# Unread products in each round of layer 0, and new times and banks for the pieces of both layers

## The chip, the cores and the metric

One core of one Trainium2 chip runs the whole program. The metric is the device time of one execution in microseconds (us); lower is better. Before the change it was 1562.08 us, the median of three runs (1560.22 to 1565.09).

## What is computed

The input is 8 batches of 512 tokens of width 256, in fp32. Two transformer layers follow each other, each with two residual steps of a normalized branch:

```python
x = x + _layernorm(_L0_attn_ref(_layernorm(x, axis=-1), ...), axis=-1)
x = x + _layernorm(_L0_ffn_ref(_layernorm(x, axis=-1), ...), axis=-1)
x = x + _layernorm(_L1_attn_ref(_layernorm(x, axis=-1), ...), axis=-1)
x = x + _layernorm(_L1_ffn_ref(_layernorm(x, axis=-1), ...), axis=-1)
```

Layer 0 is causal attention with 16 heads of 16 and rotary positions, softmax with a true row maximum, an output product with bias, and then `silu(x @ wg.T) * (x @ wu.T)` times `wd` with 768 hidden columns. Layer 1 is causal attention with 16 heads of 64 whose scores go through `50 * tanh(s / 50)`, and then a mix of each token with the one before it, a sigmoid gate `r`, and `relu(k)**2` times a weight. Nothing of the result may be dropped: all products are of fp32 quality, each computed as three products of high and low halves (`product`, line 422).

## The kernel before, in words

**Pieces and rounds.** Each layer is a function (`phase1` for layer 0, the one behind it for layer 1). The work of one batch is cut into named pieces: `x_T` (transposes of the normalized input, line 1091), `rope`, `roped`, `turned`, `rope_sum`, `rope_hi`, `rope_lo` (queries and keys with rotary positions, and their halves), `place` (12 small DMAs that put a 64-row part into the operands `l_qT` and `l_kT`, line 761), `max` and `rmax` (a first pass of the scores, lines 1118 and 1125, whose row maxima DVE takes, lines 979 and 985), `maxT` and `maxT_out` (transposed maxima, line 1154), `maxima` (two DMAs that put them into `l_qT`, line 768), `score`, `tail` and `exp` (the scores again, line 1164, with their exponentials on ACT, line 897), `pv` (probabilities times values, line 1194), `pv_out` (its copy into `l_outT`, line 991), `outT` (transposed back, line 1203) and `outT_norm` (lines 996 and 999), `att_T` (line 1214), `o` and `o_out` (the output product, and the bias added on DVE, line 1017), the norms, `x1_T`, `gate`, `up`, `hidden`, `down`, `x2`, and the DMAs `load_x` (line 774), `store` (line 778) and `residual` (line 783). Scores of layer 1 are at line 1933, its query and key products split into halves by `qk_hi` (line 1665, ACT) and `qk_lo` (line 1750, DVE), and `L360` is where SP loads a weight of layer 1.

**What sets the order.** Each piece has a time in units (24 to a round) in a table written by hand, `table`. `Schedule` sorts the pieces of each engine by it. A piece's time divided by 24 says by how many rounds it lags behind its batch, so a round holds pieces of three or four batches. Rounds 3 to 6 are one hardware loop on each engine, whose order is that of `table`; the rounds before and after are written out, in the order of `moved_table`. `loading_table` and `prologue_table` order the weights' loading and splitting before each layer, and the prologue of layer 1 is interleaved with the last rounds of layer 0. In the profile a round of layer 0 takes about 80 us (rounds 3 to 6 lie in about 280 to 600) and one of layer 1 about 100 us. The tables give order alone: an engine's program is the sorted list, and only semaphores make it wait.

**Banks.** PSUM has eight banks, and `bank_table` names the one that each piece fills. `Banks` derives the waits: before PE fills a bank, `claim` makes it wait until the piece that filled it last has been read.

**Unread products.** `heat` multiplies a weight with itself into a bank that nobody reads:

```python
def heat(nc, out, w, count):
    for _ in range(count):
        nc.tensor.matmul(out, w[:, 0, 0:P], w[:, 0, 0:T], start=True, stop=True)
```

Before the change `warm` issues it 16 times with two products each while the first weights load, and layer 1 issues it nine times with six products each (`end_heat`), for the last batch. None is issued in the rounds between.

**Waits that matter here.** All DMAs of these pieces are issued by SP in one queue of its own order. `store` waits for `x2` (POOL, line 846); `residual` waits until the store of the batch before has landed, since both use `l_x`; DVE's addition of the residual (line 1030) waits for it. `maxima` waits for `maxT_out` on ACT, and PE's `score` waits until `maxima` has landed. `load_x` waits for both `x_T` of the batch before. A weight's load waits for a staging place, or in the prologue of layer 1 for room that layer 0 still holds.

Of the kernel before, what the change touches and what calls it, by code (L numbers as in the profile page):

```python
# [29 lines left out]
NC = D // P  # L30
# [413 lines left out]
def phase1(nc, block, ctx, memory, a, x_mid, tok, banks, psum, ident, expo):  # L444
# [56 lines left out]
    with nc.sbuf_tensor("l0_staging", [P, 2 * NM, T], F32, side="right") as raw:  # L501
# [21 lines left out]
        "rope_lo": {(0,): -6.92, (1,): -4.1, (2,): 3.46, (3,): 6.47},
        "place": {(0,): 1.92, (1,): 9.15, (2,): 16.42, (3,): 17.53},
        "v": {(0,): 9.07, (1,): 10.47},
        "v_out": {(0,): 10.27, (1,): 10.78},
        "max": {(0, 0): 2.31, (0, 1): 3.12, (1, 0): 3.69, (1, 1): 4.05, (2, 0): 6.471, (2, 1): 7.51, (3, 0): 7.73, (3, 1): 8.88, (4, 0): 13.38, (4, 1): 14.18, (5, 0): 15.1, (5, 1): 16.17, (6, 0): 18.88, (6, 1): 20.29, (7, 0): 20.74, (7, 1): 21.38},
        "rmax": {(0, 0): 2.58, (0, 1): 2.81, (1, 0): 3.44, (1, 1): 4.55, (2, 0): 7.24, (2, 1): 7.7, (3, 0): 8.1, (3, 1): 9.14, (4, 0): 13.04, (4, 1): 13.17, (5, 0): 14.54, (5, 1): 15.68, (6, 0): 17.52, (6, 1): 21.61, (7, 0): 22.25, (7, 1): 22.65},
        "score": {(0, 0): 7.67, (0, 1): 8.61, (1, 0): 12.13, (1, 1): 14.05, (2, 0): 14.44, (2, 1): 16.04, (3, 0): 16.75, (3, 1): 17.84, (4, 0): 20.19, (4, 1): 20.7, (5, 0): 23.53, (5, 1): 25.98, (6, 0): 27.92, (6, 1): 29.64, (7, 0): 30.36, (7, 1): 31.2},
        "exp": {(0, 0): 9.44, (0, 1): 9.6, (1, 0): 16.13, (1, 1): 16.21, (2, 0): 16.76, (2, 1): 17.89, (3, 0): 19.08, (3, 1): 20.41, (4, 0): 22.38, (4, 1): 22.97, (5, 0): 27.35, (5, 1): 27.9, (6, 0): 29.7, (6, 1): 30.56, (7, 0): 31.05, (7, 1): 33.42},  # L530
        "mask": {(0,): 8.92, (1,): 10.92, (2,): 13.92, (3,): 17.45, (4,): 21.07, (5,): 24.91, (6,): 29.58, (7,): 29.82},
        "maxT": {(0,): 6.78, (1,): 12.031, (2,): 18.41, (3,): 25.43},
        "maxT_out": {(0,): 8, (1,): 13.44, (2,): 20.04, (3,): 27.37},
# [8 lines left out]
        "o": {(0,): 34.98, (1,): 35.71},
        "o_out": {(0,): 34.7, (1,): 35.63},
        "x1_T": {(0,): 40.61, (1,): 41.76},
        "x1_T_hi": {(0,): 42.78, (1,): 43.5},
        "x1_T_lo": {(0,): 40.69, (1,): 41.47},
        "o_stats": {(): 35.95},
        "o_rstd": {(): 32.68},
        "residual": {(): 42.28},
        "o_norm": {(): 37.14},  # L550
        "x1_stats": {(): 37.76},
        "x1_rstd": {(): 35.87},
        "x1_norm": {(): 39.24},
        "gate": {(0,): 42.98, (1,): 44.65, (2,): 47.03, (3,): 47.92, (4,): 50.99, (5,): 52.33},
# [6 lines left out]
        "down": {(0,): 54.57, (1,): 55.571, (2,): 55.612, (3,): 55.733},
        "x2_stats": {(): 56.36},
        "x2_rstd": {(): 54.86},
        "x2_norm": {(): 56.48},
        "x2": {(): 56.6},
# [1521 lines left out]
```

## Time and profile before

| what | value |
|---|---|
| median of three runs | 1562.08 us |
| the profiled execution's own time | 1562.13 us |
| its span | 1560.4 us |
| mean granted TensorE clock | 0.965 of full speed |
| share of the span busy: PE, DVE, ACT, POOL | 93%, 74%, 51%, 53% |
| DMA | 60.84 MB, mean 39 GB/s |

The own time is 0.05 us above the median, and 1.7 us more than the span; the difference lies around the span. A busy share is a mean over the whole program. The granted clock is printed per slice or stretch as a share of full speed: 1.00 is 2.4 GHz and 0.50 is 1.2 GHz. The matmul rows give the time from start to end of a group of equal instructions on one line.

### The profile page before, as it was taken

How to read it: one execution, taken by the hardware profiler on the slowest of the kernel's cores; microseconds unless marked ns; L12 is line 12 of the kernel's file. 1: busy time of each engine (PE TensorE's matmuls, PEld its weight loads, DVE VectorE, ACT ScalarE, POOL GpSimd, SP SyncE). 2: the span in 40 equal slices, each digit the busy share in tenths (PEclk: the TensorE clock that was granted, in tenths of full speed). 3: DMA queues.
4: the chain of work that ended last, by engine and by line, in shares of the span. 5: the costliest groups of instructions: out<-in, count | busy, mean ns of one | idle time of the engine just before them, and what ended most of it. 6: DMA issues, size and time to landing. Idle time of an engine off the chain costs nothing.

```text
span 1560.4 us, 29738 instructions
## 1 busy us (share of the span) xinstructions
PE 1450.1 (93%) x10854; PEld 1062.3 (68%) x10854; DVE 1153.0 (74%) x1844; ACT 799.7 (51%) x1132; POOL 831.5 (53%) x1003
## 2 busy tenths in 40 slices
PE   4878989899999997999999999999999999999997
PEld 3546666676666666677776776777767777767765
DVE  5679697878788886766657668778697687874875
ACT  2344344353435343645665656556566566565651
POOL 4143445353535453436656666566676565756652
PEclk9679999999999998999999999999999999999998
DMA  7341333333333335101100010100101001000000
GB/s 171 67 63 25 56 77 47 69 55 68 54 68 54 68 41 122 41 29 42 56 7 1 1 41 1 41 1 1 40 0 36 5 0 40 0 0 28 1 28 14
DMA packets 47268, 60.84 MB, mean 39 GB/s; under 512 B 5296, under 2 KB 32848, under 8 KB 47184
## 3 DMA queue, kind: packets, MB, share of 16 engines
q1 hardware_dynamic: 46320, 59.03, 18.5%
q8 instruction: 56, 0.92, 0.2%
q10 hardware_dynamic: 864, 0.66, 0.1%
q14 instruction: 28, 0.23, 0.1%
HBM read 25.83 MB, written 8.39 MB: 22 GB/s over the span
## 4 chain that ended last, share of the span: by engine, by line
PE 47%; POOL 17%; issue 16%; DVE 11%; DMA 4%; ACT 3%; SPq 2%; POOLq 0%; ACTq 0%; DVEq 0%
PE psum L422 23%; PE psum L1968 4%; POOL l_probs L301 4%; PE psum L1933 4%; POOL l_keysum L1602 4%; PE psum L1194 3%; POOL l_keysum L1604 3%; PE psum L1164 3%; PE psum L1984 2%; POOL l_attT_lo L1610 2%; DVE l_rowmax L979 2%; PE psum L1118 2%; DMA l_qT<-l_roped_hi 2%; DVE l_att L1759 2%; PE psum L1956 2%
## 5 line engine op out<-in xcount | busy, mean ns | idle before, releaser
L1675 ACT ACTIVATE l_probs<-psum 128x1024 f32<-128x1024 f32 (+1 forms) x192 | 164.0, 879 | 168.1 <-PE psum L1933 151.8
L1759 DVE RECIPROCAL l_att<-psum 128x512 f32<-128x512 f32 x64 | 214.5, 3352 | 47.9 <-PE psum L1956 39.8
L897 ACT ACTIVATE l_probs<-psum 128x512 f32<-128x512 f32 x256 | 138.2, 594 | 168.6 <-PE psum L1164 160.7
L979 DVE TENSOR_REDUCE l_rowmax<-psum 128x2 f32<-128x1024 f32 (+2 forms) x192 | 159.4, 862 | 48.2 <-PE psum L1125 47.9
L301 POOL TENSOR_SCALAR_AFFINE_SELECT l_probs<-l_probs 128x256 f32<-128x256 f32 (+1 forms) x384 | 186.8, 520 | 0.0
L1681 ACT ACTIVATE l_probs<-l_probs 128x2048 f32<-128x2048 f32 (+1 forms) x128 | 160.6, 1267 | 0.8
L1750 DVE TENSOR_TENSOR l_qk_lo<-psum,l_qk_hi 128x1024 fp32r<-128x1024 f32 x64 | 77.2, 1212 | 112.2 <-ACT l_qk_hi L1665 112.1
L1968 PE MATMUL psum<-l_probs,l_v 128*64 128x512 f32 (+3 forms) x1024 | 150.5, 436 | 1.0 <-DVE l_att L1765 1.0
L296 POOL TENSOR_TENSOR l_pool_holder<-expo 128x1 f32<-128x1 f32 x128 | 31.6, 247 | 186.7 <-ACT l_probs L1681 118.2
L1968 PEld LDWEIGHTS psum<-l_probs,l_v 128*64 128x64 f32 x1024 | 70.4, 137 | 88.5 <-issue 78.5
L410 POOL TENSOR_TENSOR l_x_rstd<-l_x_veps,expo 128x4 f32<-128x4 f32 (+1 forms) x50 | 53.2, 1064 | 140.7 <-DVE l_x_veps L403 140.6
L1610 POOL TENSOR_TENSOR l_attT_lo<-l_att,l_attT_hi 128x512 fp32r<-128x512 f32 x64 | 88.6, 1386 | 64.6 <-ACT l_attT_hi L1693 64.6
L1602 POOL TENSOR_TENSOR l_keysum<-l_probs 128x768 f32<-128x768 f32 x62 | 114.3, 1844 | 5.8
L1164 PE MATMUL psum<-l_qT,l_kT 64*128 64x384 f32 (+3 forms) x512 | 84.7, 394 | 24.9 <-ACT l_probs L897 11.0
L840 POOL TENSOR_TENSOR l_hT_lo<-l_gated,l_hT_hi 128x512 fp32r<-128x512 f32 x48 | 61.9, 1289 | 81.5 <-ACT l_hT_hi L920 81.5
L1118 PE MATMUL psum<-l_kT,l_qT 63*128 63x384 f32 (+3 forms) x512 | 78.4, 364 | 27.7 <-issue 13.3
L1933 PE MATMUL psum<-l_qk_hi 64*128 64x512 f32 (+3 forms) x512 | 95.6, 368 | 6.1 <-ACT l_probs L1675 3.6
L1665 ACT ACTIVATE l_qk_hi<-psum 128x1024 fp32r<-128x1024 f32 x64 | 65.6, 1026 | 64.1 <-PE psum L422 58.6
L1604 POOL TENSOR_TENSOR l_keysum<-l_keysum,l_probs 128x512 f32<-128x512 f32 x62 | 87.3, 1408 | 4.9
L823 POOL TENSOR_TENSOR l_roped_lo<-l_straight,l_turned 128x512 f32<-128x512 f32 x32 | 41.2, 1288 | 90.8 <-DVE l_turned L972 90.8
L1194 PE MATMUL psum<-l_probs,l_v 128*32 128x512 f32 (+3 forms) x1024 | 85.1, 477 | 2.4 <-ACT l_probs L897 2.3
L1933 PE MATMUL psum<-l_qk_lo,l_qk_hi 64*128 64x512 f32 (+3 forms) x512 | 83.2, 318 | 0.0
(210 smaller groups left out, 4175.9 us busy)
## 6 DMA issues: line engine op xcount, KB each, us to landing
l_kT<-l_roped_hi SPq DMA_DIRECT2D x64, 128.0 KB, 4.2
l_qT<-l_roped_hi SPq DMA_DIRECT2D x64, 128.0 KB, 5.1
l_xin<-in_x SPq DMA_DIRECT2D x8, 512.0 KB, 4.1
l_kT<-l_roped_lo SPq DMA_DIRECT2D x32, 128.0 KB, 5.2
l_qT<-l_roped_lo SPq DMA_DIRECT2D x32, 128.0 KB, 5.0
l_x<-in_x SPq DMA_DIRECT2D x8, 512.0 KB, 4.0
x_mid<-l_x SPq DMA_DIRECT2D x8, 512.0 KB, 3.0
l_xin<-x_mid SPq DMA_DIRECT2D x8, 512.0 KB, 4.9
```

Of the source, the lines that this page charges most:

```text
L301: nc.gpsimd.affine_select(out=part, in_=part, compare_op=ALU.is_ge, fill=0.0, base=0, pattern=[[0, part.shape[1]], [1, P]], channel_multip ...
L422: last = nc.tensor.matmul(out, l(c), r(c), start=(k == 0), stop=(k == len(todo) - 1))
L897: space.free(nc.scalar.activation(probs[:, SLOT[p], e, c0:c1], space.unit(*use), ACT.Exp, scale=HD0 ** -0.5), *use)
L979: reduced = nc.vector.tensor_reduce(rowmax[:, a // 2, :, a % 2, t], space.unit("max", a, k)[:, :, c0:c0 + (t + 1) * P], mybir.AxisListType ...
L1194: last = nc.tensor.matmul(space.unit("pv", g)[32 * j:32 * j + 32, kt * P:T], v0[:, kt, h * VSTEP:h * VSTEP + 32], probs[:, SLOT[p], j % 2, ...
L1602: nc.gpsimd.tensor_tensor(total, tile0, tile1, ALU.add).then_inc(summed.sem, 1)
L1604: nc.gpsimd.tensor_tensor(total[:, :, P:3 * P], total[:, :, P:3 * P], tile2, ALU.add).then_inc(summed.sem, 1)
L1675: space.free(nc.scalar.activation(probs[:, p % 2, :, c0:c1], space.unit("score", p, u)[:, :, 0:c1 - c0], ACT.Tanh, scale=HD1 ** -0.5 / CLA ...
L1681: nc.scalar.activation(part, part, ACT.Exp, scale=CLAMP).then_inc(exped.sem, 1)
L1759: space.free(nc.vector.reciprocal(att[p % 2][:], space.unit("den", p)), "den", p)
L1933: last = nc.tensor.matmul(space.unit("score", p, u)[:, e, c0:c0 + T - kt * P], l[half, slot, 1, kt * P:(kt + 1) * P], r[half, slot, 0, kt ...
L1968: last = nc.tensor.matmul(space.unit("pv", p)[64 * e:64 * e + 64, kt * P:T], v1[:, kt, 2 * p + e, :], probs[:, p % 2, e, OFF1[kt]:OFF1[kt] ...
```

## The change

It adds a piece `heat` to layer 0, six times per batch, of two unread 128x512 products of the first gate and up weight (`wgu[0]`) each, 96 products in all. It gives every piece of both layers a new time, and in the banks it moves `score` (4, 0, 0) of layer 0 from 4 to 5, `qk` (1) of layer 1 from 4 to 3, and the unread products. Each new `heat` waits for its bank, and for seven split weights, which only matters in the first batch. The diff, cut to what the text behind it speaks of (the first group is `table`, the second `moved_table` of layer 0, then the banks, the code, and tables of layer 1; the tables' other lines are left out):

```diff
+ROUND_HEATS = 6
...
-        "x_rstd": {(): -18.74},
...
-        "place": {(0,): 1.92, (1,): 9.15, (2,): 16.42, (3,): 17.53},
...
-        "maxima": {(0,): 12.68, (1,): 20.66, (2,): 24.69, (3,): 35.25},
...
-        "outT_norm": {(0,): 19.77, (1,): 24.46, (2,): 32.05, (3,): 32.58},
...
+        "x_rstd": {(): -18.24},
...
+        "place": {(0,): 4.72, (1,): 9.72, (2,): 16.86, (3,): 17.02},
...
+        "maxima": {(0,): 11.41, (1,): 19.86, (2,): 24.13, (3,): 34.64},
...
+        "outT_norm": {(0,): 20.71, (1,): 24.4, (2,): 31.68, (3,): 33.1},
...
+        "heat": {(0,): 32.781, (1,): 38.98, (2,): 33.88, (3,): 32.88, (4,): 37.5, (5,): 33.79},
...
-        "load_x": {(0,): -62.56, (1,): -53.97, (2,): 13.81, (3,): 63.81},
...
-        "maxima": {(0, 0): -2.48, (0, 1): 47.01, (0, 2): 64.88, (0, 7): 199.42, (1, 0): 16.74, (1, 1): 55.26, (1, 2): 71.998, (1, 7): 217.03, (2, 0): 29.49, (2, 1): 58.12, (2, 6): 168, (2, 7): 228.33, (3, 0): 40.28, (3, 1): 64.77, (3, 6): 185.4, (3, 7): 234.5},
...
-        "store": {(0,): 71.03, (5,): 206.3, (6,): 239.7, (7,): 263.47},
...
+        "heat": {(0, 0): 38.05, (0, 1): 57.56, (0, 6): 181.91, (0, 7): 231.66, (1, 0): 31.88, (1, 1): 23.48, (1, 6): 185.3, (1, 7): 241.84, (2, 0): 31.26, (2, 1): 60.41, (2, 6): 179.83, (2, 7): 229.11, (3, 0): 40.89, (3, 1): 68.23, (3, 6): 181.17, (3, 7): 230.45, (4, 0): 25.01, (4, 1): 33.65, (4, 6): 181.171, (4, 7): 249.3, (5, 0): 37.79, (5, 1): 60.6, (5, 6): 186.3, (5, 7): 230.76},
...
+        "load_x": {(0,): -62.48, (1,): -76.94, (2,): 16.83, (3,): 54.79},
...
+        "maxima": {(0, 0): -13.35, (0, 1): 39.3, (0, 2): 64.33, (0, 7): 197.93, (1, 0): 12.49, (1, 1): 55.67, (1, 2): 71.998, (1, 7): 224.46, (2, 0): 25.8, (2, 1): 58.32, (2, 6): 168, (2, 7): 225.56, (3, 0): 36.3, (3, 1): 64.1, (3, 6): 189.37, (3, 7): 228.19},
...
+        "store": {(0,): 67.93, (5,): 202.45, (6,): 236.8, (7,): 264.81},
...
+        "heat": {(0,): 4, (1,): 6, (2,): 5, (3,): 4, (4,): 7, (5,): 5},
...
-        "warm": {(0,): 0, (1,): 1, (2,): 4, (3,): 7, (4,): 6, (5,): 6, (6,): 2, (7,): 6, (8,): 7, (9,): 7, (10,): 2, (11,): 5, (12,): 5, (13,): 6, (14,): 4, (15,): 3},
+        "warm": {(0,): 2, (1,): 5, (2,): 0, (3,): 4, (4,): 5, (5,): 3, (6,): 3, (7,): 5, (8,): 6, (9,): 3, (10,): 5, (11,): 4, (12,): 7, (13,): 6, (14,): 7, (15,): 3},
...
-    filling = schedule.uses("x_T", "rope", "max", "max_tail", "pv", "outT", "maxT", "v", "score", "tail", "att_T", "o", "x1_T", "gate", "up", "down")
+    filling = schedule.uses("x_T", "rope", "max", "max_tail", "pv", "outT", "maxT", "v", "score", "tail", "att_T", "o", "x1_T", "gate", "up", "down", "heat")
...
-    space = Banks(psum, schedule, uses, first, WIDTH0, sem, late=("down",), unread=("warm",),
+    space = Banks(psum, schedule, uses, first, WIDTH0, sem, late=("down",), unread=("heat", "warm"),
...
+        def warm_round(i, n):
+
+            split_weights(i, FRONT + NC + 1)
+            space.claim(pe, i, "heat", n)
+            heat(nc, space.unit("heat", n), wgu[0], 2)
...
-        program(pe, {"warm": warm, "x_T": x_T, "rope": rope, "v": v,
+        program(pe, {"warm": warm, "heat": warm_round, "x_T": x_T, "rope": rope, "v": v,
...
-        "load_x": {(0,): 224.76, (1,): 253.99, (2,): 290.05, (3,): 305.95},
...
+        "load_x": {(0,): 228, (1,): 250.46, (2,): 278.66, (3,): 308.84},
...
-        "load": {(0,): 221.86, (1,): 229.19, (2,): 214.44, (3,): 203.64, (4,): 236.55, (5,): 239.15, (6,): 255.24, (7,): 244.9, (8,): 274.95, (9,): 262.25},
...
+        "load": {(0,): 220.85, (1,): 227.62, (2,): 215.12, (3,): 225.73, (4,): 230.91, (5,): 235.15, (6,): 251.86, (7,): 248.63, (8,): 274.74, (9,): 267.35},
...
-        "qk": {(0,): 0, (1,): 4, (2,): 0, (3,): 4, (4,): 2, (5,): 2, (6,): 4, (7,): 2},
+        "qk": {(0,): 0, (1,): 3, (2,): 0, (3,): 4, (4,): 2, (5,): 2, (6,): 4, (7,): 2},
...
-        "end_heat": {(0,): 4, (1,): 0, (2,): 2, (3,): 5, (4,): 0, (5,): 4, (6,): 3, (7,): 1, (8,): 2},
+        "end_heat": {(0,): 0, (1,): 4, (2,): 5, (3,): 3, (4,): 2, (5,): 1, (6,): 0, (7,): 1, (8,): 2},
```

Most times move by less than one place. What comes of them in the order of the engines, worked out from the sorted tables:

- **PE, each loop round of layer 0.** heat (0) and heat (3) come behind `max` (3, 1) and ahead of `outT` (3) of the batch before; heat (5) and heat (2) behind `v` (0) and ahead of `att_T` (0); heat (4) behind `max` (4, 0) and ahead of `tail` (0); heat (1) behind `max` (5, 0) and ahead of `rope` (0). Six pairs of other pieces change places: `score` (1, 0) goes ahead of `maxT` (1), `tail` (3) ahead of `score` (7, 1), `score` (3, 0) ahead of `x1_T` (0), `up` (0) ahead of `gate` (0), and the like.
- **POOL, each loop round.** `x_rstd` moves behind `mask` (6) and `mask` (7).
- **SP, layer change.** Before: place (3) of batch 7, load (3) of layer 1, store of batch 5, residual of batch 6, load (2), maxima (1) of batch 7, load (0), load_x of layer 1, maxima (2). After: place (3), store of batch 5, load (2), residual of batch 6, load (0), maxima (1), maxima (2), load (3), load (1), load_x.
- **SP, first rounds.** maxima (1) of batch 0 goes ahead of load_x of batch 2.
- **PE, first rounds.** `maxT` (3) and `tail` (2) of batch 1 go ahead of `max` (0, 0) of batch 2; the new pairs of batches 0 and 1 lie in rounds 1 and 2, and the `warm` pairs take other places among the loading.
- **PE, layer 1.** Neighbours change places (`o` with `score` or `v`, `den` with `pv`). Of the nine `end_heat`, two instead of one lie ahead of the last `x3_T`, and three instead of four ahead of the last `key`.

## Rows read from the trace of the kernel before

**Rows 1.** The page: busy us and share of engines, PEclk in 40 slices

```profile
PE 1450.1 (93%) x10854; PEld 1062.3 (68%) x10854; DVE 1153.0 (74%) x1844; ACT 799.7 (51%) x1132; POOL 831.5 (53%) x1003
...
PEclk9679999999999998999999999999999999999998
```

**Rows 2.** Stretches: us, busy (count) PE, PEld, DVE, ACT, POOL, clock, DMA, GB/s

```profile
360.00:440.00 80.00, 74.90 (x646) 54.34 (x641) 65.23 (x132) 35.13 (x68) 37.63 (x51) 0.96 0.36 59
...
1080.00:1180.00 100.00, 98.95 (x690) 72.38 (x689) 76.42 (x94) 60.39 (x68) 65.51 (x71) 1.00 0.05 16
```

**Rows 3.** Stretches: one place of rounds 2 to 6, then the layer change

```profile
215.00:223.00 8.00, 6.55 (x54) 2.96 (x54) 7.63 (x14) 2.33 (x5) 3.65 (x9) 0.57 0.20 68
...
296.00:304.00 8.00, 6.22 (x66) 3.47 (x64) 7.79 (x19) 2.97 (x7) 5.06 (x10) 1.00 0.00 1
...
376.00:384.00 8.00, 7.20 (x48) 3.36 (x46) 6.57 (x17) 0.92 (x2) 3.64 (x6) 0.57 0.00 0
...
454.00:462.00 8.00, 7.21 (x42) 4.18 (x46) 7.79 (x20) 2.77 (x6) 5.05 (x10) 0.57 0.01 1
...
536.00:544.00 8.00, 6.92 (x66) 3.99 (x66) 7.79 (x21) 1.80 (x4) 3.43 (x5) 0.79 0.00 0
...
611.00:623.00 12.00, 5.85 (x48) 3.23 (x52) 6.96 (x19) 5.11 (x10) 3.55 (x10) 0.57 0.52 178
...
618.00:622.00 4.00, 4.00 (x32) 2.48 (x36) 2.45 (x6) 2.02 (x4) 0.00 (x0) 0.50 0.41 141
```

**Rows 4.** Timeline of PE, round 4: start, us, what, [idle before <-releaser]

```profile
363.97 1.06 PE L1214 MATMUL psum<-ident,l_att 128*128 128x128 f32 x8 [0.61 <-DVE l_att L999]
...
374.03 0.56 PE L1164 MATMUL psum<-l_qT,l_kT 64*128 64x128 f32 x4 [0.83 <-ACT l_probs L897]
...
376.97 0.80 PE L422 MATMUL psum<-l_xT_hi,l_wqk_hi 128*128 128x512 f32 x1 [0.80 <-ACT l_probs L897]
```

**Rows 5.** Timeline of DVE: o added, outT copied, in rounds 3 and 4

```profile
292.36 0.69 DVE L1017 TENSOR_TENSOR l_att<-psum,l_b_o 128x512 f32<-128x512 f32 x1
...
304.35 0.68 DVE L991 COPY l_outT<-psum 128x512 f32<-128x512 f32 x1
...
370.58 0.69 DVE L1017 TENSOR_TENSOR l_att<-psum,l_b_o 128x512 f32<-128x512 f32 x1
...
383.87 0.69 DVE L991 COPY l_outT<-psum 128x512 f32<-128x512 f32 x1 [1.22 <-PE psum L1194]
```

**Rows 6.** Timeline of PE: unread products at the program's end

```profile
1523.42 1.55 PE L429 MATMUL psum<-l_wrkv_hi 128*128 128x512 f32 x6
...
1534.52 8.43 PE L429 MATMUL psum<-l_wrkv_hi 128*128 128x512 f32 x24 [0.69 <-ACT l_xs L1716]
```

**Rows 7.** Timelines at the layer change: POOL, SP's queue, PE, DVE

```profile
600.73 2.39 POOL L846 TENSOR_TENSOR l_x<-l_x,l_gated 128x1024 f32<-128x1024 f32 x1 [2.08 <-DVE l_gated L414]
...
606.74 0.43 SPq L778 DMA_DIRECT2D x_mid<-l_x  x1
...
613.09 1.45 SPq L768 DMA_DIRECT2D l_qT<-l_maxT  x2
...
629.83 1.30 SPq L768 DMA_DIRECT2D l_qT<-l_maxT  x2
...
617.94 0.79 PE L1164 MATMUL psum<-l_qT,l_kT 64*128 64x512 f32 x2 [5.49 <-DMA l_qT<-l_maxT]
...
639.07 1.39 DVE L397 BATCH_NORM_STATS2 l_x_stats<-l_xin 128x6 f32<-128x256 f32 x4
```

**Rows 8.** Timeline of PE in the first rounds

```profile
66.45 0.79 PE L1164 MATMUL psum<-l_qT,l_kT 64*128 64x512 f32 x2 [1.38 <-DMA l_qT<-l_maxT]
...
172.09 0.80 PE L1118 MATMUL psum<-l_kT,l_qT 63*128 63x512 f32 x2 [3.07 <-issue]
```

**Rows 9.** Timelines of layer 1: DVE's two qk_lo, then PE's first score

```profile
1099.79 2.34 DVE L1750 TENSOR_TENSOR l_qk_lo<-psum,l_qk_hi 128x1024 fp32r<-128x1024 f32 x2
...
1104.22 0.51 PE L1933 MATMUL psum<-l_qk_hi 64*128 64x512 f32 x2
```

More of the change, by code:

```diff
@@ L530, in phase1 @@
[L530 to L533, printed above, removed]
@@ L542, in phase1 @@
[L542 to L554, printed above, removed]
@@ L561, in phase1 @@
[L561 to L565, printed above, removed]
-        "store": {(): 66.03},
-        "max_tail": {(0,): 5.67, (1,): 10.35, (2,): 16.59, (3,): 22.4},
-        "rmax_tail": {(0,): 6.53, (1,): 10.38, (2,): 16.281, (3,): 22.98},
-        "tail": {(0,): 13.29, (1,): 18.93, (2,): 27, (3,): 31.241},
-        "exp_tail": {(0,): 15.51, (1,): 21.02, (2,): 29.261, (3,): 32.12},
+        "load_x": {(): -23.17},
@@ new lines, in phase1 @@
+        "o": {(0,): 34.9, (1,): 35.67},
+        "o_out": {(0,): 34.54, (1,): 35.53},
+        "x1_T": {(0,): 40.63, (1,): 41.11},
+        "x1_T_hi": {(0,): 42.85, (1,): 43.741},
+        "x1_T_lo": {(0,): 41.1, (1,): 41.33},
+        "o_stats": {(): 35.93},
+        "o_rstd": {(): 33.58},
+        "residual": {(): 43.35},
+        "o_norm": {(): 37.05},
+        "x1_stats": {(): 37.68},
+        "x1_rstd": {(): 36.521},
+        "x1_norm": {(): 39.77},
+        "gate": {(0,): 43.31, (1,): 44.5, (2,): 46.86, (3,): 47.9, (4,): 50.96, (5,): 52.56},
@@ L1385, in phase2 @@
-        "out": {(): 47.33},
-        "gate_b": {(): 71},
-        "gate": {(): 46.29},
-        "x4_stats_b": {(): 86.81},
-        "x4_stats": {(): 47.29},
-        "x4_rstd_b": {(): 90.8},
-        "x4_rstd": {(): 46.54},
-        "x4_norm_b": {(): 90.35},
-        "x4_norm": {(): 48.19},
-        "store_b": {(): 89.67},
-        "store": {(): 37.84},
+        "load_x": {(): -24},
+        "x_stats": {(): -20.44},
+        "x_rstd": {(): -20.07},
+        "x_norm": {(): -3.7},
+        "x_T": {(0,): -0.55, (1,): -0.49},
@@ L1396, in phase2 @@
+        "key_out": {(): 42.67},
+        "square": {(): 44.74},
+        "kact_hi": {(): 43.86},
+        "kact_lo": {(): 45.17},
+        "out": {(): 47.41},
+        "gate_b": {(): 70.61},
+        "gate": {(): 45.72},
+        "x4_stats_b": {(): 94.42},
+        "x4_stats": {(): 47.27},
+        "x4_rstd_b": {(): 93.61},
+        "x4_rstd": {(): 47.58},
+        "x4_norm_b": {(): 91.46},
+        "x4_norm": {(): 48.2},
+        "store_b": {(): 93.12},
+        "store": {(): 40.92},
     }
```

407 lines of the change are left out of this document (207 added, 200 removed), and 17 rows, old and new, of the table moved_table.

## The prediction, made before the changed kernel was run

> **What bounds the kernel now.** I read the page first. PE is busy for 93% of the span, and no other engine for more than 74% [rows 1], so what counts is what PE does, what it waits for, and its clock. The row of the granted clock shows low slices at the start, and single dips (an 8) later on [rows 1]. The stretches tell the two layers apart [rows 2]. A round of layer 0 has 74.90 us of PE work in 80 us: 5.10 us of waits. A round of layer 1 has 98.95 in 100 at full clock: nothing short of less PE work can shorten it, but a new wait would recur in eight batches.
>
> Next the dips, by stretches at the same place of each round [rows 3]. In rounds 2, 4 and 5 a stretch of 8 us was granted 0.57, and in round 6 0.79; round 3 has 1.00 there. A share of 0.57 over 8 us means 6.9 us at the lower level, 1.2 GHz; 0.79 means 3.4 us. Ahead of the fall of round 4 PE had waited several times but briefly: 0.83 us at 374.03 and 0.80 us ahead of 376.97, both for ACT's exponentials [rows 4]. At the layer change 12 us were granted 0.57, of which 618 to 622 were full of work at the lower level [rows 3]; ahead of them lies a wait of 5.49 us for the maxima's DMA [rows 7].
>
> **What a fall costs.** DVE adds the output product and later copies `l_outT`, with the same pieces between, in each round. In round 3, without a fall, that took 304.35 − 292.36 = 11.99 us, in round 4, with one, 383.87 − 370.58 = 13.29, and DVE there waited 1.22 us for PE, which it did not in round 3 [rows 5]. So a full fall costs 1.3 us, and the half one of round 6 about 0.65. All falls of rounds 2 to 6 are worth 3 × 1.3 + 0.65 = 4.6 us, a small sum beside the round.
>
> **What an unread product costs.** Six in a row took 1.55 us, and the record of a single 512-column product is about 0.39 long, so one more costs (1.55 − 0.39) / 5 = 0.232 us at full clock [rows 6]. 24 in a row that began at the lower level took 8.43 us, 0.35 each [rows 6]. All 96 would cost 22.3 us if none lay in a wait.
>
> **The change, part by part.**
>
> *Unread products in the loop.* Heat (0), (3), (5) and (2), eight products, stand in the stretch from `outT` (3) to `att_T` (0): 8 × 0.232 = 1.86 us. PE's only wait there is the 0.61 us ahead of `att_T` at 363.97 [rows 4]. So `att_T`, `o`, the bias on DVE and all that follows on DVE up to `x1_T` come up to 1.86 − 0.61 = 1.25 us later. The other end is zero, if the 5.10 us of waits in a round [rows 2] take it all up later. I take 1.1, near the dense end: DVE is in a chain behind `o`, and its copy of `l_outT` starts there without any wait in round 3 [rows 5]. Four loop rounds: **+4.4**. Heat (4) and (1), 4 × 0.232 = 0.93 us, stand where PE waits for exponentials (the 0.83 and 0.80 us of [rows 4] are two such waits): nothing; without that cover, 0.93 per round.
>
> *Unread products outside the loop.* 24 of the 48 pairs. Bounds are 0 and 24 × 0.46 = 11.1 us. Rounds 1, 2 and 7 have fewer batches in flight and more waits, so I take three pairs in dense stretches: **+1.4**.
>
> *The clock.* The pairs give PE work ahead of each place where it fell. Bounds for rounds 2 to 6 are 0 and 4.6; heats (4) and (1) fill only part of the short waits, so I take three quarters: **−3.4**. In round 1, where the clock is lowest [rows 1], few pairs stand and PE mostly waits: **−0.6**, half of one fall, between 0 and a few us.
>
> *Layer change, SP's queue.* `x2` was ready at 600.73 + 2.39 = 603.12, but SP stood at load (3) of layer 1, which waits for room, and issued the store at 606.74: 3.62 us late [rows 7]. The residual waits until the store has landed, maxima (1) stood behind the residual, at 613.09, and PE waited 5.49 us for it [rows 7]. Now the store goes ahead of load (3), which is issued after maxima (2). The gain lies between 0 and 3.62; two loads of 512 KB now share the queues with the store and the residual, so **−2.4**, two thirds. In return load (3), load (1) and load_x now stand behind maxima (2), which SP issued at 629.83 to 631.13. Three issues later, by about 632.4 at 0.43 each, load_x is out, and DVE reads its data at 639.07 [rows 7]: some 6.7 us to land, so nothing; with slower transfers up to a few us on DVE, not on PE's path at once. With PE's long wait shortened and four pairs of unread products of batch 6 ahead of it, the 4 us of work at the lower level [rows 3] would take 2: **−2.0**, between 0 and 2.
>
> *First rounds.* maxima (1) no longer waits behind load_x, which waits for `x_T`. PE waited 1.38 us for it at 66.45 [rows 8]; between 0 and 1.38, **−0.9**. In round 1 PE stood 3.07 us ahead of `max` (0, 0) of batch 2 at 172.09 [rows 8]; 1.3 us of other work (`maxT`, `tail`) now goes ahead of it: **−1.3**, and 0 if that work isn't ready.
>
> *POOL's x_rstd* goes behind two masks, for which PE's chain waits through the exponentials; no wait of PE names POOL in these rows: nothing. The swaps of neighbours in layer 0: nothing, as each pair of pieces is ready when its turn comes.
>
> *The end.* Three groups of six instead of four lie ahead of the last `key`. Six products fewer are 6 × 0.35 = 2.1 us, but `key` waits for its operands too; **−0.5**, between 0 and 2.1.
>
> *Layer 1.* `qk` (1) moves into bank 3, so the first score, which fills that pair of banks, must wait for DVE's `qk_lo` (1). That ended at 1099.79 + 2.34 = 1102.13, and the score began at 1104.22 [rows 9]: 2.1 us of slack, cost nothing. If that cover went, each microsecond would count eight times. The other swaps hardly touch a full PE [rows 2]: nothing.
>
> **Sum.** 4.4 + 1.4 − 3.4 − 0.6 − 2.4 − 2.0 − 0.9 − 1.3 − 0.5 = −5.3. Against the profiled execution's own 1562.13 us (0.05 above the median, so the same) that is **1556.8 us**.
>
> **The rivals.**
>
> *A, slower: PE is full and the products cost what they take.* Place: between `outT` (3) and `tail` (0) of each loop round. All twelve products then cost 12 × 0.232 = 2.8 us, 11.1 in four rounds, with 1.4 outside, and the clock falls as before. Only the 5.1 us of SP's queue, first rounds and end remain: 1562.1 + 12.5 − 5.1 = **1569.5**. It decides from the point where more than 42 of the 96 products cost their full time (9.8 us, the 5.1 and the bound of 4.7 below). For it: 74.90 of 80 us are busy, and the wait ahead of `att_T` is only 0.61. Against it: 5.10 us of waits remain in a round.
>
> *B, no change: the clock isn't recovered.* The falls come from something else than these waits, or from waits which the pairs don't fill. Without −3.4, −0.6 and −2.0 the sum is 1562.1 + 0.7 = **1562.8**. For it: the pairs ahead of `att_T` stand 10 us before the fall, in a stretch that is already full, and round 3 did without a fall and without pairs. The trace has the clock of round 4 fall after waits each under 1 us [rows 4]. The Trainium skill (TensorE: Matmul & The Clock Gate, Why this matters for your kernels) asks only that there be no long unbroken idle gap between matmuls; by it no dip of rounds 2 to 6 should exist, and products that fill short waits could bring nothing. The trace disagrees with it, by the 0.57 that follows those short waits. The same page's section on a second failure mode (psum-queue depth-cycling) tells of a clock that moves up and down where PE idles briefly and often, and the trace agrees with that.
>
> *C, a larger gain.* The pairs cost nothing, because the chain has slack later in the round, and all falls go: 1556.8 − 5.8 − 1.2 = **1549.8**. For it: DVE and ACT are busy for 65.23 and 35.13 us of 80 [rows 2], neither is full.
>
> *D, the change hardly acts*: a pair runs while PE would wait, the clock stays, SP's order is hidden. That is within 0.3% too.
>
> **How the numbers follow.** 0.3% (4.7 us) is about what a measurement of this kernel can tell from no change, so faster means under 1557.4, slower over 1566.8. The forecast has 0.40, of which 0.10 falls within 0.3%, since it lies just at the bound; C 0.17; B 0.18; D 0.05; A 0.20. Faster 0.30 + 0.17 = 0.47, same 0.10 + 0.18 + 0.05 = 0.33, slower 0.20. Cases of both signs hold most of the chance, so the forecast's own range is 1553 to 1561. The range of all reaches below C by the other ends of the waits at the layer change and at the start (1545) and up into A (1568), and leaves out most of A and a little of C.
>
> **What would show it.** Right: the granted clock of the stretch behind `o_out` is 1.00 in rounds 4 and 5; `att_T` comes 1.0 to 1.3 us later after `outT` (3) than before; SP issues the store of the layer change about 3 us earlier and PE's wait of 5.49 us shrinks by two or more; rounds of layer 1 stay at 100 us. Wrong: clocks of 0.57 remain (B); the loop's rounds take over 2 us more than before (A); or `o`'s chain is no later at `x1_T`, with the clock up (C). A change of layer 1's round by over 0.3 us would refute the zero on which eight batches rest.

## The result, and the profile after

The changed kernel takes **1568.43 us** (median of 20 runs, 1564.51 to 1569.28), the one before in the same comparison 1562.43 (20 runs). The ratio is 1.0035, with a 95% interval of 1.0029 to 1.0042: 5.5 us **slower**, where 5.3 us faster was forecast, and just outside the range of 1545 to 1568. The profiled execution took 1567.92 us, with a span of 1566.2, 5.8 more than before.

The page of the changed kernel, the same two parts as in [rows 1]:

```profile
PE 1469.1 (94%) x10950; PEld 1075.1 (69%) x10950; DVE 1131.8 (72%) x1844; ACT 799.2 (51%) x1132; POOL 822.7 (53%) x1003
...
PEclk9788999999999999999999999999999999999998
```

PE has its 96 products more and 19.0 us more of busy time. The single dips of the clock in the middle are gone. The stretches of the changed kernel say where (the columns are those of [rows 2]; the places are moved by what the kernel is late there):

```profile
360.00:440.00 80.00, 75.72 (x661) 55.89 (x660) 64.92 (x133) 35.22 (x68) 38.03 (x52) 1.00 0.36 59
1080.00:1180.00 100.00, 99.18 (x694) 73.36 (x692) 75.10 (x93) 60.83 (x70) 65.56 (x72) 1.00 0.05 16
220.00:228.00 8.00, 7.18 (x48) 3.63 (x52) 6.86 (x12) 2.66 (x5) 2.92 (x7) 0.57 0.20 68
...
384.00:392.00 8.00, 6.85 (x88) 4.17 (x83) 7.79 (x20) 2.71 (x6) 5.28 (x9) 1.00 0.00 0
462.00:470.00 8.00, 6.37 (x61) 3.76 (x64) 7.79 (x20) 3.15 (x6) 5.44 (x10) 1.00 0.01 1
544.00:552.00 8.00, 6.87 (x78) 4.19 (x78) 7.79 (x21) 2.50 (x5) 4.78 (x8) 1.00 0.00 0
618.00:630.00 12.00, 9.73 (x93) 6.01 (x92) 11.72 (x33) 5.98 (x12) 6.16 (x10) 1.00 0.29 94
```

Rounds 4, 5 and 6 and the layer change, which had 0.57, 0.57, 0.79 and 0.57 [rows 3], now have 1.00 throughout. Round 2 still has 0.57. By the forecast's prices that is 3.3 of the 4.6 us of rounds 2 to 6, three quarters as forecast, and all of the layer change. The time did not come back.

**Where the time went** is read from pieces that each batch has once. POOL's `x2` of batch 1 ends the first rounds. The row of the kernel before:

```profile
285.12 2.36 POOL L846 TENSOR_TENSOR l_x<-l_x,l_gated 128x1024 f32<-128x1024 f32 x1 [2.08 <-DVE l_gated L414]
```

The row of the changed kernel:

```profile
291.21 2.39 POOL L850 TENSOR_TENSOR l_x<-l_x,l_gated 128x1024 f32<-128x1024 f32 x1 [2.08 <-DVE l_gated L415]
```

So it is 6.1 us late before the first loop round has done anything. The same subtraction at other pieces gives +8.8 at `att_T` (0) of batch 6 (early in round 7, behind the loop), +5.2 at the last `x2` (after the layer change), +4.6 at the last `x3_T`, and +5.8 at the end. By stretch: first rounds **+6.1**, loop of layer 0 **+2.7**, layer change **−3.6**, layer 1 **−0.6**, end **+1.2**. Of the loop's 2.7 us, 2.5 have come by `att_T` of round 4, that is within the first of its rounds, where the kernel before had no fall to win back; in those behind, where it had, only 0.2 more is lost.

### The profile page after: what moved, and what is told of

Read it like the earlier page. It is cut to its first block, busy times and chain, and to the rows that moved or that the text cites. A ratio compares the mean times of both kernels' runs of the same rounds, so it can differ in the third digit from the quotient of the medians.

```text
span 1566.2 us, 29953 instructions
## 1 busy us (share of the span) xinstructions
PE 1469.1 (94%) x10950; PEld 1075.1 (69%) x10950; DVE 1131.8 (72%) x1844; ACT 799.2 (51%) x1132; POOL 822.7 (53%) x1003
## 4 chain that ended last, share of the span: by engine, by line
PE 56%; POOL 17%; issue 13%; DVE 9%; ACT 3%; DMA 1%; SPq 1%; POOLq 0%; ACTq 0%; DVEq 0%
PE psum L423 28%; PE psum L1198 5%; POOL l_probs L302 4%; PE psum L1978 4%; POOL l_keysum L1612 4%; PE psum L1943 4%; PE psum L1168 3%; POOL l_keysum L1614 3%; PE psum L1122 3%; PE psum L1994 2%; DVE l_rowmax L983 2%; PE psum L430 2%; PE psum L1966 2%; POOL l_attT_lo L1620 2%; DVE l_att L1769 1%
## 5 line engine op out<-in xcount | busy, mean ns | idle before, releaser
L297 POOL TENSOR_TENSOR l_pool_holder<-expo 128x1 f32<-128x1 f32 x128 | 28.0, 219 | 276.2 <-ACT l_probs L1691 195.0
L1620 POOL TENSOR_TENSOR l_attT_lo<-l_att,l_attT_hi 128x512 fp32r<-128x512 f32 x64 | 85.0, 1330 | 41.0 <-ACT l_attT_hi L1703 40.9
L1168 PE MATMUL psum<-l_qT,l_kT 64*128 64x128 f32 (+3 forms) x512 | 82.9, 388 | 13.8 <-ACT l_probs L901 10.1
L1614 POOL TENSOR_TENSOR l_keysum<-l_keysum,l_probs 128x512 f32<-128x512 f32 x62 | 83.0, 1339 | 4.9
L1198 PE MATMUL psum<-l_probs,l_v 128*32 128x512 f32 (+3 forms) x1024 | 80.2, 456 | 4.5 <-POOL l_probs L302 2.2
```

Of the source, the lines that this page charges most:

```text
L1198: last = nc.tensor.matmul(space.unit("pv", g)[32 * j:32 * j + 32, kt * P:T], v0[:, kt, h * VSTEP:h * VSTEP + 32], probs[:, SLOT[p], j % 2, ...
L1614: nc.gpsimd.tensor_tensor(total[:, :, P:3 * P], total[:, :, P:3 * P], tile2, ALU.add).then_inc(summed.sem, 1)
```

## The experiments

All times are medians against runs of the kernel before on the same chip; of the ratio 0.001 is 1.6 us. The first four ask whether the unread products or the orders lose the time.

**1. No unread products in the rounds**, the orders as changed:

```diff
         def warm_round(i, n):
 
+            return
             split_weights(i, FRONT + NC + 1)
```

> The changed kernel without its 96 unread products of layer 0; all orders and banks as changed. Theory 1 (the loss of about 6 us comes from the new order of the first rounds, and the products in the loop are paid back by the clock): 1565 to 1568 us, the stretches at the lower clock of rounds 4 to 6 are back, and batch 2's x2 is still 5 us or more later than in the kernel before. Theory 2 (the products cost more than the clock gives back, in the loop or outside): 1558 to 1563 us, and batch 2's x2 is at most 2 us later.

Measured: 1567.97, ratio 1.0041 (1.0027 to 1.0056). The products are not the loss: without them the kernel is as slow. In its trace batch 1's `x2` is 6.3 us late, and the lower clock is back at places of rounds 3 to 5 and at the layer change. Its mean granted clock is 0.967, against 0.977 with them, at the same time.

**2. Products in the hardware loop alone** (`if isinstance(i, int): return` in the same place):

> The changed kernel with the unread products of layer 0 in the hardware loop alone (rounds 3 to 6), none in the rounds written out. If the products of the first rounds cost the loss: 3 to 5 us less than the changed kernel, about 1564. If it is the order of the first rounds: within 1.5 us of the changed kernel, about 1568. The clock of rounds 3 to 6 stays at 1.00 either way.

Measured: 1565.18, ratio 1.0019 (1.0005 to 1.0032), but spread from 1559.37 (mean clock 0.980) to 1569.77 (0.970). The profiled execution was that slowest one. By the ratios it is 2.5 us under the changed kernel, and the spread overlaps both readings, so the time settles nothing about the products outside the loop. The trace says more: it has none in the first rounds, and batch 1's `x2` is 7.2 us late all the same. Its clock falls to 0.79 in one stretch of round 5, where 1.00 was expected. Beside run 1, which differs by the loop's products alone, the ratio is 0.0022 lower, 3.4 us: in this pair they cost nothing.

**3. Products outside the loop alone** (`if not isinstance(i, int): return`):

> The changed kernel with the unread products of layer 0 outside the hardware loop alone. If the products in the loop pay for themselves by the clock, within 1.5 us of the changed kernel (1567 to 1570), with stretches at the lower clock in rounds 4 to 6 and rounds as long as with them. If they cost 1.1 us a round on top, 4 us less than the changed kernel (1564); if the clock gives more than they take, 2 us or more slower (1570).

Measured: 1566.33, ratio 1.0031 (1.0019 to 1.0043). By the ratios that is 0.6 us under the changed kernel: the loop's products pay for themselves, or nearly.

**4. The old orders with products in the loop.**

> The kernel before, with the six pairs of unread products in the hardware loop alone, at the changed kernel's times for them; all other orders and banks as before. If the products pay for themselves by the clock: within 1.5 us of the kernel before (1561 to 1564), granted clock 1.00 in rounds 4 to 6. If they cost 1.1 us a round and the clock gives back less: 1565 to 1567. If the clock gives more than they take: under 1560.

Measured: 1572.93, ratio 1.0078 (1.0065 to 1.0091), 12 us slower and outside all that was expected. The profiled execution was its fastest (1566.47, mean clock 0.971); the four others had 0.961 to 0.965. In the trace of that one the clock is 1.00 throughout rounds 4 to 6, and the lag of `x2` grows by 2.0 us from batch 1 to batch 4, about what the forecast's prices give. The median lies 6.5 us above that execution, so some 6 us of the 12 lie in what the four slower executions do otherwise; the mean clock of the kernel before was 0.963 to 0.970 in the same comparison, so it didn't rise with the products there. Where it fell in those four no trace shows.

**5. and 6. The first rounds by themselves.** The changed kernel with the old times for all pieces of layer 0's rounds 0 to 2 and the loading, and without the unread products of these rounds; and the reverse, the kernel before with the new times, without products. (That products there are not the loss, runs 1 and 2 have shown.) One of the lines that go back in the first:

```diff
-        "load_x": {(0,): -62.48, (1,): -76.94, (2,): 16.83, (3,): 54.79},
+        "load_x": {(0,): -62.56, (1,): -53.97, (2,): 13.81, (3,): 63.81},
...
+            if isinstance(i, int) and i < 2:
+                return
```

> The changed kernel with the orders of the kernel before in layer 0's rounds 0 to 2 and in the loading (their unread products left out, the warming pairs in their old banks); all from round 3 on as changed. Theory 1 (the new order of the first rounds is the loss): 5 to 7 us less than the changed kernel, 1561 to 1563, and batch 1's x2 within 1 us of the kernel before (it was 6.1 late). Rival (the loss only shows there, but is caught up by waits later anyway): within 2 us of the changed kernel.

Measured: 1562.34, ratio 0.9992 (0.9983 to 1.0001). The loss is gone, and batch 1's `x2` stands 0.6 us from where it stood before the change.

> The kernel before with the changed orders in layer 0's rounds 0 to 2 and in the loading alone, without unread products in the rounds. Theory 1: 5 to 7 us slower than the kernel before, 1567 to 1569, with batch 1's x2 6 us later. Rival: within 2 us of the kernel before.

Measured: 1565.71, ratio 1.0018 (1.0009 to 1.0027), 2.8 us slower; batch 1's `x2` is at 288.41, 3.3 late. So the new orders of the first rounds cost about 3 us in the old kernel and about 6 in the new one. The timeline shows both parts. In round 2 of this kernel PE waits twice in one spot:

```profile
215.44 0.49 PE L1118 MATMUL psum<-l_kT,l_qT 63*128 63x512 f32 x2 [1.39 <-DMA l_qT<-l_roped_hi]
...
219.06 0.79 PE L1118 MATMUL psum<-l_kT,l_qT 63*128 63x384 f32 x4 [2.62 <-DVE l_xT_lo L959]
```

In the kernel before it waits once:

```profile
216.35 0.79 PE L1118 MATMUL psum<-l_kT,l_qT 63*128 63x384 f32 x4 [1.91 <-DVE l_xT_lo L959]
```

That is 4.01 against 1.91, 2.1 us more: the placement of batch 2's queries is now waited for. The other 3 us lie in round 1. The stretch there (PE, PEld, DVE, ACT, POOL, clock), first of kernel 6:

```profile
131.00:142.00 11.00, 8.21 (x88) 5.40 (x87) 10.71 (x25) 3.67 (x8) 4.49 (x10) 1.00 0.07 24
```

and of the changed kernel:

```profile
131.00:142.00 11.00, 9.73 (x64) 4.80 (x62) 8.94 (x23) 3.15 (x6) 4.45 (x10) 0.53 0.07 25
```

PE is busier at 0.53 and gets 64 matmuls done instead of 88. Its timeline there, the new unread products among it:

```profile
133.44 2.07 PE L430 MATMUL psum<-l_wgu_hi 128*128 128x512 f32 x4
...
137.76 4.31 PE L1198 MATMUL psum<-l_probs,l_v 128*32 128x512 f32 x32 [0.21 <-ACT l_probs L901]
```

and the same `pv` in kernel 6:

```profile
134.59 2.36 PE L1194 MATMUL psum<-l_probs,l_v 128*32 128x512 f32 x32 [0.57 <-ACT l_probs L897]
```

At 132.3 both kernels are at the same piece to 0.1 us; at `pv` the changed one is 3.2 later, and `pv` takes 2 us more. The kernel of run 1, without products, also falls to the lower clock there (134 to 144), so the products don't cause that fall, but once it is there four of them cost 2.07 us. Nor is the fall tied to the program: run 13 below is the changed kernel up to the layer change, products and banks included, and its profiled execution, the fastest of six, has the full clock there. Its stretch, and its `x2` of batch 1:

```profile
131.00:142.00 11.00, 9.48 (x91) 5.78 (x91) 10.85 (x25) 3.70 (x8) 5.12 (x10) 1.00 0.13 45
```

```profile
288.19 2.39 POOL L850 TENSOR_TENSOR l_x<-l_x,l_gated 128x1024 f32<-128x1024 f32 x1 [2.08 <-DVE l_gated L415]
```

The four products take 1.19 us in that trace, and `x2` is 3.1 us late, as in kernel 6 (3.3). The changed kernel's two traces and those of runs 1, 2, 3, 9 and 14, whose first rounds differ from it at most by the products or one DMA, all have 0.53 to 0.75 in that stretch, and an `x2` that is 6.1 to 7.2 us late. So the changed kernel's 6.1 are about 3 us of waits that the new orders bring, and about 3 us of a fall in round 1 which most executions have. The kernel before isn't free of it either: 0.84 in the same stretch. What decides whether it comes is open.

**7. The new order in layer 1's hardware loop alone.** Example of its lines:

```diff
-        "qk": {(0,): 1.42, (1,): 1.69, (2,): 7.52, (3,): 8.19, (4,): 14.13, (5,): 15.06, (6,): 17.22, (7,): 23.3},
+        "qk": {(0,): 1.66, (1,): 1.71, (2,): 7.46, (3,): 8.69, (4,): 14.17, (5,): 15.04, (6,): 17.36, (7,): 23.28},
```

> The kernel before with the changed order in the hardware loop of layer 1 alone (rounds 3 to 6; pieces that would change their round keep their place). If the order there is what made those rounds 0.93 us shorter: rounds of 101.33 instead of 102.27 us in the trace, and 2.5 to 4.5 us less in all, 1558. If the shorter rounds came from the bank of qk (1) or from the pieces that change their round: rounds stay at 102.27, and the time at 1562.

Measured: 1558.87, ratio 0.9971 (0.9959 to 0.9982), 4.5 us **faster**. The round is read between two `x3_T`, first of the kernel before:

```profile
1048.73 0.49 PE L1995 MATMUL psum<-ident,l_xn 128*128 128x128 f32 x3
...
1151.00 1.03 PE L1995 MATMUL psum<-ident,l_xn 128*128 128x128 f32 x8
```

and of this one:

```profile
1048.01 1.03 PE L1995 MATMUL psum<-ident,l_xn 128*128 128x128 f32 x8
...
1149.32 0.92 PE L1995 MATMUL psum<-ident,l_xn 128*128 128x128 f32 x7
```

102.27 us has become 101.31, three times over; the step into the loop, from the `x3_T` ahead of it, has gone from 104.45 to 103.62. The stretch of 100 us of this kernel, beside that of [rows 2]:

```profile
1080.00:1180.00 100.00, 99.20 (x691) 72.84 (x690) 76.03 (x93) 60.84 (x69) 65.50 (x72) 1.00 0.05 16
```

By the starts in PE's timeline 0.7 of it is in the 96 products of `o`, which take 12.3 instead of 13.0 us. The bank of `qk` (1) is as before here, so it plays no part.

**8. The store ahead of load (3) at the layer change**, nothing else:

```diff
-        "load": {(0,): 221.86, (1,): 229.19, (2,): 214.44, (3,): 203.64, (4,): 236.55, (5,): 239.15, (6,): 255.24, (7,): 244.9, (8,): 274.95, (9,): 262.25},
+        "load": {(0,): 221.86, (1,): 229.19, (2,): 214.44, (3,): 228.4, (4,): 236.55, (5,): 239.15, (6,): 255.24, (7,): 244.9, (8,): 274.95, (9,): 262.25},
```

> The kernel before with load (3) of layer 1's weights behind maxima (2) of batch 7 in SP's order, so that the store of batch 5 no longer waits behind it; nothing else. If the forecast's term was right: the store is issued 3 us or more earlier, PE's wait of 5.49 us for the maxima shrinks by 2 to 3.6, and the time is 2 to 3 us less, 1559. If the store's data or the maxima themselves are late anyway: within 1 us.

Measured: 1558.19, ratio 0.9961 (0.9949 to 0.9973), 6 us faster, twice what was expected. Timelines of SP's queue and PE, and the stretch (columns as above):

```profile
603.50 0.39 SPq L778 DMA_DIRECT2D x_mid<-l_x  x1
...
608.55 1.45 SPq L768 DMA_DIRECT2D l_qT<-l_maxT  x2
...
613.42 0.50 PE L1164 MATMUL psum<-l_qT,l_kT 64*128 64x512 f32 x2 [0.85 <-DMA l_qT<-l_maxT]
```

```profile
608.00:620.00 12.00, 7.46 (x86) 4.71 (x84) 11.76 (x32) 8.24 (x16) 6.15 (x10) 1.00 0.51 175
```

The store goes out 3.24 us earlier, the maxima 4.54, since the residual between them also follows the store sooner (4.06 us behind it instead of 5.37), and PE's wait shrinks from 5.49 [rows 7] to 0.85. With the long wait gone the clock stays at 1.00 where it had 0.57 [rows 3], without an unread product there. In this trace, that is: run 15 has the same order of SP and falls.

**9. load_x of batch 3 back** behind the placements, the one DMA whose move was suspected in the first rounds:

```diff
-        "load_x": {(0,): -62.48, (1,): -76.94, (2,): 16.83, (3,): 54.79},
+        "load_x": {(0,): -62.48, (1,): -76.94, (2,): 16.83, (3,): 63.81},
```

> The changed kernel with load_x of batch 3 back behind the places of batch 2 in SP's order, where it stood before, and no longer ahead of maxima (1) of batch 1. If that DMA, which waits for x_T, delays the maxima and PE's scores at 135: 1 to 2 us less than the changed kernel, about 1567, and batch 1's x2 at most 5 us late in the trace. If the first rounds lose their 6 us elsewhere (order of PE, the clock): no difference, 1568.

Measured: 1568.97, ratio 1.0044 (1.0031 to 1.0057). No gain, and batch 1's `x2` is 6.4 us late: it was not this DMA.

**10. to 12. Layer 0's loop: its new order, and the products in it.** The kernel before with the changed `table` of layer 0 (loop rounds only); the same with the products in the loop; the same with twice as many.

```diff
-            heat(nc, space.unit("heat", n), wgu[0], 2)
+            heat(nc, space.unit("heat", n), wgu[0], 4)
```

> The kernel before with the changed order in the hardware loop of layer 0 alone (rounds 3 to 6), without unread products. If the loop's order is neutral, as the forecast had it: within 1 us of the kernel before. If it makes the rounds longer: 1 us or more for each, 1565 or more.

> The same with the unread products in that loop. If they pay for themselves by the clock: within 1.5 us of the kernel without them. If each round gets the forecast's 1.1 us and the clock gives back less: 3 to 5 us above it. If in this order they hold the clock as in the changed kernel while in the old order of the loop they didn't (that kernel took 11 us more): clock 1.00 in rounds 4 to 6 in the trace and a mean clock of 0.97 or more in every run.

> The kernel with the changed order in layer 0's loop and unread products there, with four products a pair piece instead of two (24 a round instead of 12). If a product more costs its full 0.232 us everywhere: 48 x 0.232 = 11 us more than with two. If only those ahead of att_T do: 32 x 0.232 = 7.4 us more. If the clock or the waits take them up: under 4 us more.

Measured: 1563.36, ratio 1.0010 (1.0001 to 1.0018); 1565.46, 1.0023 (1.0013 to 1.0033); 1573.02, 1.0081 (1.0066 to 1.0096). The order is close to neutral. The first 48 products cost 2 us net, with the mean clock up from 0.967 to 0.970 (run 11's trace has 1.00 in rounds 4 to 6, but a mean of 0.97 or more was not reached in every execution: 0.968 to 0.973); the next 48 cost 9 us more with the clock at 0.971, between the 7.4 of those ahead of `att_T` and the 11 of all. Once the clock is up, more products are only work.

**13. and 14. The changed kernel's layer change and end.** load (3) back ahead of the store (`(3,): 225.73` to `(3,): 201.5` in `load`), and a fourth group of unread products ahead of the last `key` again (`(1, 7): 522.68` to `(1, 7): 488` in `end_heat`). The changed kernel ran with them for comparison.

> The changed kernel itself once more, on the same chip as the three others, to compare with: 1568 to 1569 us.

Measured: 1566.96, ratio 1.0037 (1.0023 to 1.0052).

> The changed kernel with load (3) of layer 1's weights back ahead of the store of batch 5. If the new SP order is what the changed kernel gains at the layer change: 3 to 5 us slower than the changed kernel, 1572. If the unread products there gain it by the clock: within 1 us.

Measured: 1570.84, ratio 1.0065 (1.0052 to 1.0079), 3.9 us over the changed kernel. So SP's order is a gain in it too, beside the products. The profiled execution was the kernel's fastest (1564.61, mean clock 0.981; the others 0.973 to 0.976), so its trace doesn't show the usual loss.

> The changed kernel with a fourth group of six unread products ahead of the last key, as before the change (the group is taken from those behind it). If PE's wait of 3.06 us there lets the clock fall, so that key's twelve products take 4.3 instead of 2.8 us: clock 1.00 over key and 1 to 1.5 us less than the changed kernel, run in the same call. If the clock falls anyway: within 0.5 us.

Measured: 1566.52, ratio 1.0030 (1.0017 to 1.0043), 0.4 us less than the changed kernel: not to be told from it in the timed runs. The traces do differ. PE at `key` and at the piece behind it, changed kernel:

```profile
1546.97 0.47 PE L423 MATMUL psum<-l_mixk_hi,l_wrkv_hi 128*128 128x512 f32 x1 [3.06 <-POOL l_mixk_lo L1626]
...
1551.30 0.36 PE L423 MATMUL psum<-l_wrkv_hi,l_mixr_hi 128*128 128x256 f32 x1
```

with four groups:

```profile
1547.36 0.48 PE L423 MATMUL psum<-l_mixk_hi,l_wrkv_hi 128*128 128x512 f32 x1 [2.38 <-POOL l_mixk_lo L1626]
...
1550.23 0.28 PE L423 MATMUL psum<-l_wrkv_hi,l_mixr_hi 128*128 128x256 f32 x1
```

`key` takes 4.33 us behind three groups and 2.87 behind four: the granted clock over it is 0.62 behind three (1547.00 to 1551.30) and 1.00 behind four (1547.00 to 1550.20). The other traces bear it out: `key` takes 4.2 to 4.4 us in all eight with three groups ahead of it, and 2.8 to 2.9 in all ten with four, and from the last `x3_T` to the end it is 29.5 to 29.8 us against 28.3 to 28.8. So the group moved away costs 1.2 us or so at the end; the timed runs agree in sign, within their noise.

**15. The two gains together**, on the kernel before (edits of runs 7 and 8):

> The kernel before with the two parts of the change that gained alone: load (3) of layer 1's weights behind maxima (2) (which gave 6 us by itself) and the changed order in layer 1's hardware loop (4.5 us by itself). If the two add up, as they lie in different stretches: 1552 to 1554. If they share a gain (the later rounds catch up what the layer change loses): 1556 to 1558.

Measured: **1554.46**, ratio 0.9953 (0.9940 to 0.9967), 7.4 us faster than the kernel before and, by the two ratios, some 13 us faster than the changed one. It has no unread product in a round. The sum of the two single gains, 0.0029 + 0.0039, would have been 10.6 us; the interval of the ratio (5.2 to 9.4 us) falls short of it, but those of the two single gains are as wide, so whether they add in full is not decided. In its trace, of the fastest execution, the layer change gains 3.5 us and layer 1's rounds 3.7. By the same reading (the lag of `x2` from batch 5 to batch 6) run 8 gained 5.4. The difference is the clock: here PE's wait for the maxima is 1.81, and the clock falls behind it.

```profile
611.66 0.79 PE L1164 MATMUL psum<-l_qT,l_kT 64*128 64x512 f32 x2 [1.81 <-DMA l_qT<-l_maxT]
```

```profile
612.00:616.00 4.00, 4.00 (x32) 2.18 (x34) 2.77 (x9) 2.29 (x5) 1.44 (x4) 0.50 0.37 128
```

The traces of the other kernels tell what holds the clock at the layer change. With SP's old order and no unread products there (the kernel before and runs 4, 6, 7, 10, 11 and 12) PE waits 5.4 to 6.2 us for the maxima, and the clock falls in all seven. With SP's new order and no products there it falls in three of four (runs 1, 2 and 15, not run 8). With the products there (the changed kernel twice, runs 3, 5, 9, 13 and 14) it stays at 1.00 in all seven; there they fill half of PE's longest wait, which is 1.82 us in runs 1 and 2 and 0.90 in the changed kernel. So the shorter wait alone is not enough as a rule, and the products do hold the clock, as forecast.

## Why the prediction was wrong, point by point

- **First rounds: the step that failed.** The forecast had "The swaps of neighbours in layer 0: nothing, as each pair of pieces is ready when its turn comes", and −0.9 and −1.3 for two waits removed. Outside the loop the orders are written out and differ from before in dozens of places, and I priced two. Measured: +6.1 us in the trace, 6 us in the timed runs when undone (run 5), 3 us when done alone (run 6). With its share of the clock and of the products the forecast had some −3 for this stretch, so it holds 9 of the 11 us between −5.3 and the trace's +5.8. The two waits that I priced are gone, as forecast, but others came in their place. Where PE waited 1.38 us for the maxima [rows 8], it now waits longer, for DVE:

```profile
66.46 0.65 PE L1122 MATMUL psum<-l_kT,l_qT 63*128 63x384 f32 x4 [2.11 <-DVE l_xT_lo L963]
```

  And the 1.91 us at batch 2's `max` became 1.39 + 2.62 in run 6. The second half of the loss is the clock of round 1, for which I had −0.6. Around it the clock is indeed higher than before (0.84 against 0.80 up to 130 us, 1.00 against 0.95 from 142 to 215), but the stretch 131 to 142 went from 0.84 to 0.53, and that costs about 3 us: run 13's trace has 1.00 and comes 3 us earlier. The rival A looked for the loss in the loop; none of the rivals had it here.
- **Unread products in the loop: right, by mechanism and size, in the changed order.** Batch 2's `x2` is 7.5 us late (370.88 against 363.34), and `att_T` of round 4, here in the changed kernel's PE timeline, 8.6: the lag grows by 1.1 us.

```profile
372.57 0.60 PE L1218 MATMUL psum<-ident,l_att 128*128 128x128 f32 x4
```

  The 8.6 is 372.57 − 363.97 [rows 4]; in run 1, without products, `att_T` of this round stands at 371.53, 1.0 earlier, so they are what the 1.1 is. The round gets back in the next stretch what the clock gives, as DVE's timeline shows:

```profile
379.17 0.69 DVE L1021 TENSOR_TENSOR l_att<-psum,l_b_o 128x512 f32<-128x512 f32 x1
...
390.84 0.69 DVE L995 COPY l_outT<-psum 128x512 f32<-128x512 f32 x1
```

  11.67 us instead of the 13.29 of [rows 5], 1.6 where 1.3 was forecast. Net of the clock the forecast's terms for the loop were 4.4 less three quarters of 3.3; runs 10 and 11 measure +2 between them, run 3 beside the changed kernel +0.6, and run 2 beside run 1 −3.4, with a wide spread. Run 4 doesn't fit: in the old order the same products made the program 12 us slower, and only the loop of its fastest execution (2.0 us by its trace) is near the forecast's prices. Why is open, so the size holds for the changed order alone.
- **The clock: right in the loop and at the layer change**, where all falls are gone; rival B, that it would not come back, is refuted there. A second trace of the changed kernel shows the same, but for a stretch of 0.57 in round 3. The fall of round 2 stayed, at 0.57, and round 1 lost by it instead of gaining, as said.
- **Layer change: right, by mechanism and nearly by size.** Forecast −4.4, in the trace −3.6, in which what the products there cost is contained. For its two terms: SP's order gives 3.5 us without the clock (run 15's trace) where −2.4 was forecast, and the clock 1.8 more (run 8's trace against run 15's) where −2.0 was. Timed, the order gives 3.9 in the changed kernel (run 13 against it) and 6 by itself (run 8), of which the clock has a part. The third that I took off the 3.62 for loads beside the store was wrong: PE's wait shrank by 4.6 in run 8, and in the changed kernel it is gone.
- **Layer 1: wrong.** "Nothing short of less PE work can shorten it" failed. A busy share of 99% hid a saving of 0.96 us a round, and of that only 0.25 is a rise of the busy share (98.95 [rows 2] to 99.20). It gains 3.7 us over four rounds alone (run 7). In the changed kernel most of that is given back ahead of its loop, where the lag grows by 3.5 us between the last `x2` and the second `x3_T`; 1.4 of it is `o` (2) standing in another round (108 products of `o` between the two `x3_T` instead of 96), and the rest is open. The old order in that stretch alone was not tried. The 2.1 us of slack for the bank of `qk` (1) held: no wait of the first score appears.
- **The end: wrong in sign, −0.5 forecast, +1.2 in the trace.** Fewer products ahead of `key` didn't bring it forward; it waits for POOL, and behind 3.06 us of that wait PE ran `key` at the lower clock, 1.5 us longer. The forecast had counted what six products cost and not that they fill this wait (run 14).
- **The range** reached 1568 by rival A, which had the right sign by the wrong place: PE in the loop. It would have been wide enough by 0.4 us more.

## What to carry to other kernels

When a change moves hundreds of pieces, count the places that are *not* in a loop as carefully as those that are: here the loop came out about as forecast, and the first rounds, which are written out, lost more than all gains. Split such a change before judging it: two of its parts alone make the kernel 7.4 us faster than before, while the whole makes it 5.5 slower. A higher mean clock is no gain by itself: with and without the unread products the changed kernel takes the same time, at 0.977 and 0.967.

## What the runs showed of the hardware that was not expected

- A wait's length and what fills it both reach the clock. At the layer change 5.4 to 6.2 us of waiting with nothing in it were followed by the lower clock in seven traces of seven, waits of at most 1.6 to 1.8 us in three of four, and with unread products ahead, where no wait was above 1.02 us, in none of seven. The order of SP's queue, one 512 KB load placed ahead of a store or behind it, made the first of these into the second.
- Six unread products ahead of a wait cost nothing and saved 1.5 us: `key` took 2.8 to 2.9 us in ten traces with them and 4.2 to 4.4 in eight without.
- Executions of one program differ in where the clock falls, and some orders spread more than others: run 2 lay between 1559.37 us at a mean clock of 0.980 and 1569.77 at 0.970, the changed kernel between 0.975 and 0.979. A single profile can be the fastest execution of its kernel (runs 4, 10, 13 and 15) and hide what the median shows. A fall in round 1 worth 3 us came in seven of eight traces of the changed kernel and its variants.
- Two programs whose PE is busy for 98.95% and 99.20% of the same 100 us of layer 1, at full clock, have rounds of 102.27 and 101.31 us. The busy share does not tell how much work got done in it.
